# Linear attention with routed experts on one core: attention rows accumulated into DRAM by DMA, and a reordered first stage

## What is computed

```python
x  = L0_attn_x
xn = _layernorm(x)
# gated linear attention: 8 heads, key 128, value 64, decay alpha = sigmoid((xn@Wg+bg)/16)
state = at * state + kt[..., None] * vt[:, :, None, :]
out_t = einsum('bhk,bhkv->bhv', qt, state)
attn  = (out * sigmoid(xn @ Wog)) @ Wo
# mixture of experts: 64 experts, 8 per token out of 4 of 8 groups, at most 256 tokens per expert
y   = (silu(buf @ w_gate) * (buf @ w_up)) @ w_down
ffn = scatter_add(y * weight)
x + attn + ffn
```

## Time and profile before

| | |
|---|---|
| median of 3 runs | 1388.67 us (1388.16 to 1389.8) |
| the profiled execution | 1381.22 us |
| its span, first to last instruction | 1379.6 us |
| granted TensorE clock, mean | 0.985 of full |
| PE busy | 1291.0 us (94%) |
| DVE busy | 950.1 us (69%) |
| ACT busy | 550.0 us (40%) |
| POOL busy | 503.6 us (37%) |
| DMA moved | 203.05 MB, mean 147 GB/s |

### The profile page before, as it was taken

How to read it: one execution, slowest core, us unless ns; L and a number is a source line. 1 busy time by engine, 2 the same in 40 slices (tenths; PEclk the granted TensorE clock), 3 DMA queues, 4 the chain that set the end, 5 groups by cost and what they waited for, 6 DMA issues and landing times.

```text
span 1379.6 us, 27517 instructions
## 1 busy us (share of the span) xinstructions
PE 1291.0 (94%) x9460; PEld 1132.8 (82%) x9460; DVE 950.1 (69%) x2427; ACT 550.0 (40%) x1078; POOL 503.6 (37%) x405
## 2 busy tenths in 40 slices
PE   4899999999999999899999999999999999999981
PEld 3678887888888887698888998989989888888870
DVE  4787878788786659767576675775757757668430
ACT  5555655555654433333333333333333333333220
POOL 1010010010010049525455455463645545455332
PEclk9899999999999999999999999999999999999995
DMA  6357434353342212337466565664656647566486
GB/s 219 128 203 239 143 116 158 126 174 130 127 157 86 77 47 78 104 111 171 116 177 131 158 161 130 164 144 136 161 121 166 168 108 185 112 182 159 129 272 213
DMA packets 134375, 203.05 MB, mean 147 GB/s; under 512 B 12384, under 2 KB 106144, under 8 KB 134176
## 3 DMA queue, kind: packets, MB, share of 16 engines
q1 hardware_dynamic: 108064, 160.57, 35.1%
q0 software_dynamic: 26240, 41.63, 16.7%
HBM read 152.81 MB, written 57.74 MB: 153 GB/s over the span
## 4 chain that ended last, share of the span: by engine, by line
PE 71%; DVE 9%; DMA 7%; issue 6%; ACT 3%; POOL 3%; SPq 1%; DVEq 0%; POOLq 0%; ACTq 0%
PE bank L702 17%; PE bank L785 6%; PE bank L805 6%; PE bank L827 6%; PE bank L717 5%; PE bank L752 5%; PE bank L734 5%; PE bank L770 4%; PE bank L836 4%; PE bank L773 3%; PE bank L743 3%; DMA out_dram<-arena 3%; DMA arena<-table,idx_all 2%; PE bank L817 2%; PE bank L646 2%
## 5 line engine op out<-in xcount | busy, mean ns | idle before, releaser
L569 POOL DMA_INDIRECT arena<-table,idx_all x132 | 146.4, 1109 | 319.8 <-DVE arena L1412 271.8
L577 POOL DMA_INDIRECT acc<-arena,idx_all x128 | 222.2, 1736 | 43.3 <-issue 41.0
L702 PE MATMUL bank<-xp,wq 128*128 128x512 f32 x768 | 214.7, 415 | 0.0
L702 PE MATMUL bank<-xp,wk 128*128 128x512 f32 x768 | 203.0, 399 | 0.0
L702 PEld LDWEIGHTS bank<-xp,wk 128*128 128x128 f32 x768 | 141.2, 188 | 34.1
L702 PEld LDWEIGHTS bank<-xp,wq 128*128 128x128 f32 x768 | 141.0, 190 | 27.9
L1309 DVE TENSOR_TENSOR_SCAN Dt<-decay,eye_b 128x512 f32<-128x512 f32 x128 | 155.8, 1219 | 1.8 <-DMA decay<-decay_dram 1.8
L752 PE MATMUL bank<-qT,kT 128*128 128x128 f32 x1024 | 136.0, 276 | 2.7 <-ACT kT L1007 2.7
L1007 ACT ACTIVATE qT<-bank 128x512 f32<-128x512 f32 x128 | 76.6, 598 | 142.2 <-PE bank L702 142.2
L752 PEld LDWEIGHTS bank<-qT,kT 128*128 128x128 f32 x1024 | 124.4, 192 | 5.0 <-ACT kT L1007 4.5
L785 PEld LDWEIGHTS bank<-V,kw 128*128 128x128 f32 x960 | 117.6, 191 | 11.7 <-issue 9.8
(11 more groups left out here) (153 smaller groups left out, 2244.1 us busy)
## 6 DMA issues: line engine op xcount, KB each, us to landing
decay<-decay_dram SPq DMA_DIRECT2D x64, 512.0 KB, 5.5
carry<-decay_dram SPq DMA_DIRECT2D x60, 512.0 KB, 4.9
arena<-in_L_attn_x_dram SPq DMA_DIRECT2D x16, 512.0 KB, 4.4
table<-arena SPq DMA_DIRECT2D x16, 512.0 KB, 3.0
xT_dram<-arena SPq DMA_DIRECT2D x16, 512.0 KB, 3.0
arena<-in_L_ffn_w_gate_dram SPq DMA_DIRECT2D x64, 128.0 KB
arena<-in_L_ffn_w_up_dram SPq DMA_DIRECT2D x64, 128.0 KB
arena<-in_L_ffn_w_down_dram SPq DMA_DIRECT2D x64, 128.0 KB
```

The source lines that it names most:

```text
L569: pool.indirect_dma_start(out=xg[:, e % 2, j, :], out_offset=None, in_=table[:, :], in_offset=bass.IndirectOffsetOnAxis(ap=idx_all[:, e, j ...
L577: pool.indirect_dma_start(out=acc[:, :], out_offset=bass.IndirectOffsetOnAxis(ap=idx_all[:, e, j:j + 1], axis=0), in_=yb[:, e % 2, j, :], ...
L702: last = mm(to[:, :], w[:, part, k, h * DK:(h + 1) * DK], xp[:, other, k, :], start=(k + i == 0), stop=(k == KD - 1 and i == 2))
```

## The change

Four parts.

1. **Attention rows.** `aside`, its stores, the loads, POOL's eight adds and the stores behind them are gone. In steps 7 to 14 POOL issues one accumulating DMA that adds `res` of chunk c - 1 to `acc` (512 KB). It is issued once `res` is ready and the scatter of the expert before has landed, and the step's first scatter waits until it has landed. After the last scatter SP copies chunks 0 to 13 of `acc` to the output by four DMAs from DRAM to DRAM (one per batch, 1835 KB each), with `load_carry` of pairs 2 and 3 between them; the last chunk is stored by four DMAs, one as each batch is done.
2. **First tokens.** ACT normalises two of the four batches, DVE the other two. PE transposes the two halves into banks 7 and 6 without a wait between; DVE copies them out, and ACT writes the high part from that copy.
3. **First copies and statistics.** The decays of chunk 0 and `route_groups(0)` come earlier on DVE, the split of Wog and Wo later on both engines (on ACT between the copies of step 0), and `statistics(1)` comes ahead of the scans instead of behind them.
4. **Norm steps.** PE's router for the third chunk of a step moves behind the scores of head 7, and its `decays_across` to the step's end; DVE and ACT follow. On DVE the statistics of s = 5 move behind the `At` of head 5. On ACT the square root's table load comes after a q copy, and the second `og` sigmoid one head later.

The core of the diff:

```diff
@@ SP, expert step and end
-                    wait_apart(sp, wo_cp, 4 * c)
-                    sp.dma_start(aside[c - 1 - DIRECT]..., res[:, :, :]).then_inc(res_out, 16)
...
+            def copy_out(b):
+                sp.dma_start(out[b][0:(C - 2) * P, :], acc_batch[b][0:(C - 2) * P, :]).then_inc(copied, 16)
+            copy_out(0)
             load_carry(C - 1, 2)
+            copy_out(1)
+            copy_out(2)
+            load_carry(C - 1, 3)
+            copy_out(3)
             store_res(C - 1, out_tiles[C - 2])
+            for b in range(B):
+                sp.wait_ge(wo_cp, 4 * (C - 1) + b + 1)
+                sp.dma_start(out_tiles[C - 1][:, b, :], res_end[:, b, :]).then_inc(end_out, 16)
@@ POOL
+            def add_attention(c, e):
+                pool.wait_ge(wo_cp, 4 * c)
+                if e > 0:
+                    pool.wait_ge(scattered, 16 * NHALF * e)
+                else:
+                    pool.wait_ge(init_acc, 16 * B)
+                pool.dma_start(acc_tiles[c - 1], res[:, :, :], accum_op=ALU.add).then_inc(att_added, 16)
             for e in range(E):
+                if e % STEP_E == 0:
+                    add_attention(E0 + e // STEP_E, e)
                 pool.wait_ge(y_cp, e + 1)
                 gather(e + 2)
                 if e > 0:
                     pool.wait_ge(scattered, 16 * NHALF * e)
                     pool.nop().then_inc(yb_free, 1)
+                if e % STEP_E == 0:
+                    pool.wait_ge(att_added, 16 * (e // STEP_E + 1))
                 scatter(e)
@@ PE
+ROUTED_AT = ((1, 3), (4, 3), (H, 0))
+ACROSS_AT = ((2, 1), (5, 1), (H, 3))
-                    if s % 3 == 1 and place == 3:
+                    if (s, place) in ROUTED_AT:
                         router(n)
-                    if s % 3 == 2 and place == 1:
+                    if (s, place) in ACROSS_AT:
                         decays_across(n)
@@ ACT, norm steps
-                    if s % 3 == 0 and place == (0 if s > 0 else 1):
+                    if s % 3 == 0 and place == 1:
                         std_of(n)
-                    if s in og_slots(kind) and place == 2:
+                    if s in (1, 4, 5, 7) and place == 2:
@@ DVE
+            def tokens_kept(k):
+                dve.wait_ge(xT_ps, k + 1)
+                dve.tensor_copy(xnT[:, k, :], tokens_bank(0, k)[:, :]).then_inc(xT_dve, 1)
...
-                    if s % 3 == 2 and place == 3 and not (isinstance(n, int) and n == C - 1):
+                    if s in (2, H) and place == 3 and not (isinstance(n, int) and n == C - 1):
                         statistics(n + 1)
...
+                    if s == 6 and kind == "norm":
+                        statistics(STEP_N * c + STEP_N)
```

More of the change, by code:

```diff
@@ L50 @@
 DIRECT = E0 - 1
-ASIDE = E1 - 1 - DIRECT
 N_CONSTS = 10
@@ L306, in in_turns, with tokens_bank @@
             return kind in ("slots", "experts", "last")
+        def tokens_bank(c, k):
+            return bank[6] if is_first(c) and k == 1 else bank[7]
         def og_slots(kind):
@@ L395, in load_addend @@
                     wait_apart(sp, wo_cp, 4 * (c - 1))
+                if not isinstance(c, int) or 1 < c <= E0:
                     wait_apart(sp, res_out, 16 * (c - 1))
@@ L959, in tokens @@
             def tokens(c, k):
+                if is_first(c):
+                    act.wait_ge(xT_dve, k + 1)
+                    f(xp[:, 0, k, :], xnT[:, k, :], ACT.Copy).then_inc(xT_cp, 1)
+                    return
                 act.wait_ge(xT_ps, 2 * c + k + 1)
@@ L1069, in step @@
                 qk_copy(c, kind, 0, 0)
-                if not first:
+                if first:
+                    weights_high("og")
+                else:
                     beside(c, kind, 0, 1)
@@ L1078, in step @@
                 v_copy(c, kind, 2)
+                if first:
+                    beside(c, kind, 0, 1)
+                    v_copy(c, kind, 3)
                 if kind in ("norm", "count", "slots"):
                     keys_weighted(c, 0)
-                v_copy(c, kind, 3)
+                if not first:
+                    v_copy(c, kind, 3)
                 if kind == "norm":
@@ L1421, in beside @@
                     if s == 0 and place == 3:
-                        if is_first(c):
-                            statistics(n)
-                        else:
+                        if not is_first(c):
                             route_groups(n - 1)
-                        scales(n)
+                            scales(n)
                         route_ranks(n - 1)
@@ L1435, in beside @@
                         route_weights(n - 1)
-                    if s % 3 == 1 and place == 3:
+                    if (s, place) in ((1, 3), (4, 3), (H, 1)):
                         gates(n)
@@ L1522, in step @@
                         projected(c, s - 4, kind)
-            route_groups(0)
-            for h in range(SCAN_LAG):
-                decay_scan(0, h)
+            decay_scan(0, 0)
+            decay_scan(0, 1)
+            scales(1)
+            decay_scan(0, 2)
+            decay_scan(0, 3)
             step(0, "norm")
```

99 lines of the change are left out of this document (45 added, 54 removed).

## The result

Faster: 1340.82 us median (1339.49 to 1343.04, 4 runs) against 1388.41 us (1386.26 to 1389.8, 4 runs), ratio 0.966, 95% interval 0.9642 to 0.9678. The forecast was 1344.3 in a range of 1336 to 1361. The profiled executions are 1381.22 (span 1379.6) and 1339.49 (span 1337.9), so by them the gain is 41.7 us, by the medians 47.6.

The account below looks back on a forecast made before the run. PE was taken to bound the kernel, gains coming only from its idle time and the span's ends. Tail -27, start -10, norm steps -7 and adds 0 gave 1388.7 - 44.4 = 1344.3 us, range 1336 to 1361.

Parts of the forecast that it names:

- The bound: Whole kernel: PE busy 1291.0 of 1379.6 us; gain only from its 89 us idle time and the span's ends.
- The tail: End of the span: load-add-store chain goes, copies hide behind PE's last step; -27 us.
- The term for the last store: End of the span: one 128 KB store remains, taken as 3.5 us, between 2.5 and 5.5.
- The copies at 180 GB/s: Rival at the end: slow copies hold the last step, gain 19 instead of 27, total 1352 us; chance 0.1.
- the first rival: Expert steps: adds twice as long delay gathers, costing PE 16 to 24 us, total 1360 to 1368; chance 0.13.
- Start and step 0: Span's start through step 0: earlier tokens and decays, PE's 8.8 us hole nearly gone; -10 us (-7 to -12).
- DVE's chain to the second At: Step 0: DVE's stretch from the decays to that At shrinks from 27.45 to 24.2 us, At at 44.5.
- Norm steps 1 to 4: PE's holes shrink by 1.8 us a step; -7 us (-4 to -13.5), DVE then setting these steps.
- the record's own sign: Norm steps: 78 us with DVE idle in them would show the prediction wrong; 76 to 77 us, right.
- the first closes: Norm steps: PE's 1.68 us hole, tokens waiting for ACT, was to close, though 0.4 us stay.
- The expert steps: Steps 7 to 14: the eight accumulating adds cost 0 us, with +0.7 us per step (+6) as far bound.
- The sum: Whole kernel: all terms give -44 us, profiled 1337; the 7.45 us from profile to median carried over, 1344.3.

Follow-up runs that it names:

- e11_old_tail: The changed kernel with part 1 undone (attention rows stored aside and added at the end as before); 1366.61 us, ratio 0.9878 to the kernel before.
- e8_changed: The changed kernel itself run again, unaltered, on a slower chip as base for further edits; 1345.47 us, ratio 0.9659 to the kernel before.
- e7_both: The changed kernel with DVE's norm-step loop written out and ACT copying the next tokens' first half before head 4's q and k; 1335.42 us, ratio 0.9586.
- e12_old_unrolled: The kernel before with only DVE's loop over norm steps 1 to 3 written out; 1379.76 us, ratio 0.9977.
- e1_tail: The kernel before with part 1 alone added (accumulating adds, copies at the end); 1354.54 us, ratio 0.9787.
- e9_gates_back: The changed kernel with ACT's share of part 4 undone (output gate one slot earlier, square root half a slot earlier); 1344.38 us, ratio 0.9716.
- e6_tokens_first: The changed kernel with ACT copying the first half of the next tokens before head 4's q and k copy; 1342.01 us, ratio 0.9636.
- e3_no_norm: The changed kernel without part 4, so parts 1, 2 and 3 on the kernel before; 1346.09 us, ratio 0.9735.
- e2_tail_order: The kernel before with parts 1 and 3 added, first tokens as before; 1352.12 us, ratio 0.9771.
- e4_no_adds: The changed kernel with its eight accumulating DMAs left out, so the output lacks those attention rows; 1337.18 us, ratio 0.9663.

## Why the prediction was right, and where it was wrong

- **The bound.** PE's idle time and the ends held the whole gain: PE is busy 1289.7 us after, 1291.0 before.
- **The tail: -27 forecast, -29.9 in the profiles, some 30 (0.0218 of the ratio) by e11_old_tail.** The mechanism held: the copies hid behind the last step. The term for the last store was taken as 3.5 us and is 2.2. The other 1.6 us were not foreseen: in the profile of before PE ran its last 48 matmuls at a lower clock, after not (windows of before, then of after; PE busy, PEclk, DMA share, GB/s):

```profile
1340.00:1350.00 10.00, 7.48 (x48) 0.83 0.70 230
```

```profile
1328.00:1338.00 10.00, 5.90 (x48) 1.00 0.16 52
```

  These 1.6 us come and go: e8_changed has 7.47 us at 0.83 there and an end of 71.8, e7_both 5.96 at 1.00 and 70.4.
- **The rivals of the DMAs.** The copies at 180 GB/s did not come. The adds cost next to nothing, as forecast: some 4 us of data where 4.7 were taken, and by the last six expert steps about 1.4 us in all. The scatter behind was not even held up. But the first rival's condition was nearer than its 0.13 may sound: a second add, which is its add of twice the size, brought its price and its sign, 20.7 us in the expert steps where it had 16 to 24.
- **Start and step 0: -10 forecast, -14.0 measured.** The first V projection was forecast at 16.9 and came at 15.85, the decays at 20.3 and came at 19.01, the second At at 44.5 and came at 41.92. Some 1.6 us of this is luck, the earlier arrival of Wg: e12_old_unrolled, with the old start, has its first V projection at 17.67, e1_tail at 18.19. From the end of PE's first transposes to that projection the forecast had 16.9 - 9.66 = 7.2 us, and 7.7 came (from 8.11); before had 9.4. So the new order gave 1.7 us there and not the 2.2 forecast, and the luck made it look like more. The step that was mis-sized is DVE's chain to the second At: it was to take 24.2 us and took 22.9, for one because the 0.8 us of waiting for ACT's part of Wo did not come. In the rest of the step 1.7 us were forecast and 2.9 came: the sum had one hole, and before has three there, of 1.40, 0.74 and 0.97 us. The clock is in neither term, as before's was at 1.00 behind its hole of 1.40. How much it matters shows in the kernel without part 4's place for the gate: over the medians, e9_gates_back against the changed kernel, that one hole of 1.88 us is worth nearly 8 us (0.0056 of the ratio).
- **Norm steps 1 to 4: -7 forecast, -2.2 measured.** This is the term that failed, and the record's own sign of it came: norm steps of 78 us with DVE idle in them (78.2, with 2.9 and 3.1 us of idle time). In its working, "the first closes, since a table load and a sigmoid leave the way of ACT's copy" is wrong: they left, and the wait for DVE's product with the old q, which they had covered, was still there; e6_tokens_first, which takes ACT's copy out from behind it, wins 4.1 us in these steps. And DVE's place against PE was taken as given, while the moved gates and decays push its 3 us of idle time at the loop's back edge into the output projection. The forecast 1.8 us a step is nearly what came once the loop is written out: 7.4 us for the four steps, of which 2.3 belong to the loop, by e12_old_unrolled, and 5.1 to the reorder on top. That DVE would set these steps was right. (A small slip beside it: 1.85 us before 333.13 is 331.3, not 331.1.)
- **The expert steps: 0 forecast.** The 4.4 us between the two profiles are at most in part a price of the adds: 2.1 lie in the last six steps, of which the adds explain about 1.4 on the mean, and 2.3 in the first two, where kernels without adds differ by 4.0 among themselves. The rest is not settled; the waits for gathers carry part of it, 9.8 us against 6.2 in the expert steps.
- **The sum.** -44.4 was too much against the profiled executions (-41.7) and too little against the medians (-47.6). Carrying the 7.45 us between profile and median of before over to after had no ground: after's own is 1.3. And that the sum came so near is partly luck: against the profiles, the end (2.9) and the start (4.0) gave more than forecast, the norm steps (4.8) and the expert steps (4.4) less, and these errors nearly cancel.

## What to carry to other kernels

Before a stall is priced away, list what else its queue would wait for at that moment: here a wait for DVE stood behind what was removed; it is written in the program, and the trace of before had the product ending 0.1 us before the copy. A looped step on one engine is a different program from the same step written out, so hold the two against each other in the profile (78.2 against 77.2 us here) before moving work across the back edge. And price a hole of about 2 us in a busy TensorE twice, once as idle time and once for the stretch behind it at half clock, which comes in some executions and not in others; the holes of 1.1 to 1.7 us in the norm steps of these traces were followed by a clock of 1.00.

## What the runs showed of the hardware

- A hole of 1.88 us on TensorE at 59 to 62 us was followed by a granted clock of 0.50 to 0.53 for 10 us in e3_no_norm, by some 10 us at half clock in e2_tail_order too, and by 1.00 in e9_gates_back, whose windows up to there read like those of e3_no_norm. One of 2.15 us at 33.7 us was followed by 0.83 (window of 10 us, 30 to 40) in the changed kernel and by 1.00 in e4_no_adds, where step 0 differed by 0.3 us only, since PE waited there for other engines anyway.
- VectorE stands for 2.80 to 3.15 us at the back edge of its loop over a long step, with nothing that it waits for (both edges in each of eleven kernels), and for none when the steps are written out. Why the edge takes so long was not tried.
- An accumulating DMA of 512 KB from SBUF took GpSimd 1.38 to 1.43 us to issue; its data took some 4 us, from about 2 us after the start of the issue.
- Copies from DRAM to DRAM, with a few loads between them, moved 338 GB/s on the mean over 28 us beside a busy TensorE (9.5 MB between 1290 and 1318; each copied byte counted once).
